# Nine stages fused into three blocks, the third scan's spreads reordered, gate products on half rows, and the position table loaded earlier

## The reference

```python
x = _L0(x)   # window attention (8x8 windows, 8 heads) + MLP 64-256-64 (gelu), a layernorm before each
x = _L1(x)   # bias, 12x12 FIR up by 2, leaky relu, clip, 12x12 FIR down by 2
x = _L2(x)   # selective scan over 8 tokens of each pixel, both directions; then
             #   y = (ys * gelu(z)) @ W_out ; group norm of y ; return x + y
x = _L3(x)   # see below

# _L3, with 4 chunks of 16 channels, L = 1024 pixels
xn = layer_norm(x)
xi, z = split(xn_chunk @ in_w.T)
xc = silu(causal_conv4(xi) + conv_b)
h  = exp(dt*A) * h + (dt*xc) B      # per pixel, 32 channels x 16 states
y  = (sum_s h*C + xc*Dp) * silu(z)
ym = y @ out_w.T + skip_scale * xn_chunk
tm = layer_norm(ym) @ proj_w.T + proj_b
out = x + tm
return out + fc2(gelu(fc1(out))) + x
```

## Time and profile before

| | |
|---|---|
| median of three executions | 1917.81 us (1914.59 to 1926.75) |
| the profiled execution, own time | 1923.28 us |
| its span (first to last instruction) | 1921.2 us |
| mean granted tensor clock | 0.932 of full |
| busy: PE, DVE, ACT, POOL | 1538.0, 1544.9, 1204.6, 1076.6 us |
| third scan: first to last scan of DVE starts | 1343.2 to 1811.6 us |

### The profile page before, as it was taken

One profiled execution on the slowest core, in us unless ns is written; L12 is line 12 of the kernel. 1 busy time (PEld: TensorE's weight loads), 2 busy tenths in 40 slices (PEclk: granted clock), 3 DMA queues, 4 the chain that ended last, 5 costly groups with the idle time before them and its releaser, 6 DMA issues. The chain is left out here.

```text
span 1921.2 us, 29107 instructions
## 1 busy us (share of the span) xinstructions
PE 1538.0 (80%) x9958; PEld 788.5 (41%) x9958; DVE 1544.9 (80%) x1256; ACT 1204.6 (63%) x1855; POOL 1076.6 (56%) x700
## 2 busy tenths in 40 slices
PE   5999887998887788878887876668787788777687
PEld 2666545885333333333333333234333333333233
DVE  3787655555899999999999999443999999999754
ACT  4666584435676767667767664366667766766356
POOL 1777401000577777777777775100989889888401
PEclk8999998998899999998999998778999999999799
DMA  4000000000444444444454454100000000000001
GB/s 142 3 0 0 1 1 1 1 1 1 77 93 95 92 94 93 93 94 92 87 98 91 94 97 90 37 1 1 1 1 1 0 0 0 0 0 1 12 1 44
DMA packets 23295, 78.08 MB, mean 41 GB/s; under 512 B 3776, under 2 KB 4672, under 8 KB 22976
## 3 DMA queue, kind: packets, MB, share of 16 engines
q0 software_dynamic: 18288, 66.59, 18.3%
q1 hardware_dynamic: 4944, 10.68, 1.9%
HBM read 8.58 MB, written 2.10 MB: 6 GB/s over the span
## 5 line engine op out<-in xcount | busy, mean ns | idle before, releaser
L1288 POOL TENSOR_TENSOR s_prod<-s_ahead,s_cs 128x1024 f32<-128x1024 f32 x127 | 309.1, 2434 | 185.6 <-DVE s_back L1231 157.2
L1909 POOL TENSOR_TENSOR r_state<-r_state,r_cs 128x1024 f32<-128x1024 f32 x127 | 300.7, 2376 | 187.5 <-DVE r_state L1860 187.5
L1860 DVE TENSOR_TENSOR_SCAN r_state<-r_decay,r_pu 128x1024 f32<-128x1024 f32 x128 | 292.7, 2287 | 26.9 <-PE r_py L1706 23.0
L1228 DVE TENSOR_TENSOR_SCAN s_ahead<-s_fore,s_pu 128x1024 f32<-128x1024 f32 x128 | 292.7, 2287 | 9.2 <-ACT s_fore L1145 2.3
L1231 DVE TENSOR_TENSOR_SCAN s_back<-s_aft,s_pu 128x1024 f32<-128x1024 f32 x128 | 289.5, 2262 | 1.3 <-ACT s_aft L1155 1.3
L1779 ACT ACTIVATE r_decay<-r_pd,r_aneg 128x1024 f32<-128x1024 f32 x128 | 142.8, 1116 | 122.6 <-PE r_pd L1650 122.2
L1145 ACT ACTIVATE s_fore<-s_pd,s_aneg 128x896 f32<-128x896 f32 x128 | 130.0, 1016 | 111.3 <-PE s_pd L958 110.3
L1650 PE MATMUL r_pu<-r_partsu,selr 64*128 64x512 f32 x512 | 156.7, 426 | 41.8 <-DVE r_state L1860 36.9
L1856 DVE TENSOR_TENSOR r_pu<-r_pu,r_bs 128x1024 f32<-128x1024 f32 x128 | 155.2, 1213 | 12.8 <-PE r_pu L1650 12.4
L958 PE MATMUL s_pu<-s_partsu,selr 64*128 64x512 f32 x512 | 100.0, 469 | 76.6 <-DVE s_back L1231 73.4
L1221 DVE TENSOR_TENSOR s_pu<-s_pu,s_bs 128x1024 f32<-128x1024 f32 x128 | 154.6, 1208 | 4.8 <-PE s_pu L958 4.8
(11 more groups left out here) (345 smaller groups left out, 3285.8 us busy)
## 6 DMA issues: line engine op xcount, KB each, us to landing
s_ahead<-s_back POOLq DMA_DIRECT2D x127, 512.0 KB, 4.6
x_act<-in_x_dram SPq DMA_DIRECT2D x8, 256.0 KB, 5.5
out_dram<-x_act SPq DMA_DIRECT2D x16, 128.0 KB, 2.4
k_fir<-in_pack_fir_dram SPq DMA_DIRECT2D x1, 1600.0 KB, 10.6
k_scan<-in_pack_scan_dram SPq DMA_DIRECT2D x1, 1600.0 KB, 13.9
k_l<-in_pack_l_dram SPq DMA_DIRECT2D x1, 515.0 KB, 3.5
k_l<-in_pack_l_dram SPq DMA_DIRECT2D x1, 450.0 KB, 14.6
k_ln<-in_pack_ln_dram SPq DMA_DIRECT2D x3, 131.0 KB, 2.8
```

The costliest lines, as they stand in the source:

```text
L1228: dve.tensor_tensor_scan(ahead[:, v % 4], f, feed[:], 0.0, ALU.mult, ALU.add).then_inc(ahead_done, 1)
L1288: pool.tensor_tensor(prod[:, b], ahead[:, v % 4], cs[:, buf].rearrange("p i n -> p (i n)"), ALU.mult).then_inc(prod_done, 1)
L1860: dve.tensor_tensor_scan(state[:, v % 4], decay[:, v % 4], feed[:], 0.0, ALU.mult, ALU.add).then_inc(scanned, 1)
L1909: pool.tensor_tensor(state[:, v % 4], state[:, v % 4], cs[:, phase, q // 2], ALU.mult).then_inc(multiplied, 1)
```

## The change

1. `rel` is a tensor of the first block; `load` issues its 16 transfers on SP behind x and the attention constants, ahead of the other constants. In `attention` DVE scales the query bias first and copies the table after it.
2. `gated`: each half's product uses only its own 64 rows, at its own row position of the array, and the two stand side by side with one semaphore step; four banks and four gate buffers.
3. `normed_mlp` holds n2 and m0 in one block, and n4, `project3` and m3 in another. `normed_convolve3` holds `groupnorm`, n3 and `convolve3`. Averages run one chunk behind; the first chunk is split inside the norm's loop; weights are prepared at its start; activation tables are loaded by name ahead of the loops; of the group norm's four scalings POOL makes the last two.
4. `scan3`: the eight spreads of a group move from one per step to `SLOTS`: none in steps k = 0 and 1, two in k = 2 and k = 6. `r_place` moves behind the sums, one in k = 6 and one in k = 0. ACT's Ln moves from k = 2 to k = 1.

The diff, cut to its core:

```diff
@@ attention
-            dve.wait_ge(rel_in, 16 * HALVES * WS)
+            dve.tensor_scalar(bq_scaled[:], c["bq"], float(HD) ** -0.5, None, ALU.mult).then_inc(bq_done, 1)
+            dve.wait_ge(rel_in, 16 * HALVES * WS)
             dve.tensor_copy(bias[:], rel[:, ::-1, :].rearrange("p j h -> p h j")).then_inc(bias_done, 1)
@@ gated, tensor
+            for k in range(CHUNKS + 1):
+                if k < CHUNKS:
+                    wait(pe, gate_done, 2 * k - 2)
+                    for h in range(HALVES):
+                        rows = slice(h * C, (h + 1) * C)
+                        mm = pe.matmul(ps_z[2 * k % 4 + h][:], c["wz"][rows, h * P:(h + 1) * P],
+                                       src[rows, k * N:(k + 1) * N], start=True, stop=True, tile_position=(h * C, 0))
+                    mm.then_inc(z_done, 2)
@@ normed_mlp, tensor
+            for n in range(CHUNKS + 1):
+                if n < CHUNKS:
+                    wait(pe, norm_done, n - 3)
+                    pe.matmul(center[n % 4][:], ln["center"], src[:, n * N:(n + 1) * N], start=True,
+                              stop=True).then_inc(centered, 1)
...
+                if project and n >= 3:
...
+                    pe.matmul(ps_proj[k % 2][:], c["wpj"], xn[:, k * N:(k + 1) * N], start=True,
+                              stop=True).then_inc(proj_done, 1)
@@ normed_mlp, scalar: norm loop, then
+                if n == CHUNKS - 3:
+                    high(0)
+            act.preload_act_table_set("gelu_and_others")
+            for n in range(CHUNKS):
+                if n + 1 < CHUNKS:
+                    high(n + 1)
@@ normed_mlp, vector: behind the norm of chunk n
+                if project and n >= 2:
+                    mix(n - 2)
+            if project:
+                low(0)
+                mix(CHUNKS - 2)
+                mix(CHUNKS - 1)
@@ normed_convolve3, tensor
+                    pe.wait_ge(x_done, n * N // HW + 1)
+                    wait(pe, norm_done, n - 3)
@@ normed_convolve3, vector
+            add(0)
+            add(1)
...
+            for n in range(CHUNKS):
+                if n == CHUNKS - 2:
+                    low(0)
+                    low(1)
...
+                if n in (1, 2):
+                    add(n + 1)
@@ normed_convolve3, gpsimd
+            for bl in range(2, BL):
+                pool.tensor_scalar(scaled[:, bl], src[:, bl * HW:(bl + 1) * HW], gain[:, bl:bl + 1],
+                                   offset[:, bl:bl + 1], ALU.mult, ALU.add).then_inc(scaled_late, 1)
@@ scan3
+        SLOTS = [0], [1], [2, 3], [4], [], [], [5, 6], [7]
...
-                    if k == 2 and live(s, UNITS):
+                    if slot == 5 and live(s, UNITS):
                         pe.wait_ge(lo_bc, gi + 8)
...
+                if z % 8 in (2, 4) and live(o, UNITS):
+                    phase, chunk = cells(z)[1], z % 8 // 4
+                    pe.matmul(ps_y[:], place[:, 2 * phase + chunk], xc[:, columns(o - z % 16 + 8 * chunk, N)],
+                              start=False, stop=False, skip_group_check=True)
@@ scan3, scalar, k == 1
+                    act.wait_ge(one_done, gi + 8)
+                    act.activation(ln[:], one[:], ACT.Ln).then_inc(ln_done, 8)
```

More of the change, by code:

```diff
@@ L1415, in _ @@
[L1415 to L1422 removed]
+            act.wait_ge(const_in, 16)
@@ new lines, in _ @@
+            act.preload_act_table_set("gelu_and_others")
+            for n in range(CHUNKS):
+                if n + 1 < CHUNKS:
+                    high(n + 1)
+                wait(act, tot_done, n - 1)
+                for unit in range(4):
+                    k = unit % 2
+                    act.wait_ge(hid_done, 4 * n + unit + 1)
+                    act.activation(act_out[:, n % 2, unit], hidden[unit][:], ACT.Gelu,
+                                   bias=c["b1"][:, k:k + 1]).then_inc(gelu_done, 1)
@@ L1444, in convolve3, with low @@
-def convolve3(nc, consts, xn, xc):
+            dve.wait_ge(ln_in, 16)
+            dve.wait_ge(w1_hi, 1)
+            dve.tensor_tensor(w1[:, 1], c["w1"], w1[:, 0].bitcast(F32), ALU.subtract).then_inc(w1_lo, 1)
+            dve.tensor_tensor(bias[:], c["b2"], c["l1b"], ALU.add).then_inc(bias_done, 1)
+            def low(n):
+                dve.wait_ge(hi_done, 2 * n + 2)
+                wait(dve, hid_done, 4 * (n - 1))
+                for h in range(HALVES):
+                    split(dve, hidden_src[:, n * N:(n + 1) * N], parts[:, n % 2, h], h, True).then_inc(lo_done, 1)
@@ L1446, in convolve3, with _, normed_convolve3 @@
+        @block.gpsimd
+        def _(pool):
+            if project:
+                for n in range(CHUNKS):
+                    cols = slice(n * N, (n + 1) * N)
+                    pool.wait_ge(mixed_done, n + 1)
+                    pool.tensor_tensor(x[:, cols], mixed[:, cols], x[:, cols], ALU.add).then_inc(resid_done, 1)
+def normed_convolve3(nc, consts, src, sums, x, xn, xc):
     with ExitStack() as ctx:
         m = Scope(nc, ctx)
+        g, g_in = consts["l2post"]
+        ln, ln_in = consts["ln"]
@@ L1453, in convolve3 @@
+        centered, squared, var_done, logged, rstd_done, norm_done, out_done = (
+            m.sem("c_" + t) for t in ("centered", "squared", "var", "logged", "rstd", "norm", "out"))
         folded_done, w_hi, w_lo, zeroed, hi_done, lo_done, conv_done, silu_done = (
@@ L1692, in body @@
                         wait(pe, y_done, o - 1)
-                    if z % 8 == 3:
-                        for chunk in range(2):
-                            pe.matmul(ps_y[:], place[:, 2 * phase + chunk],
-                                      xc[:, columns(o - z % 16 + 8 * chunk, N)], start=False, stop=False,
-                                      skip_group_check=True)
                     if isinstance(o, int) and o == UNITS - 1:
@@ L1938, in _, with load @@
             skewed3(pool, body)
-def load(block, dram, x, arrived, consts, tiles):
+def load(block, dram, x, arrived, consts, tiles, rel, rel_in):
     @block.sync
```

464 lines of the change are left out of this document (248 added, 216 removed).

## The result

The changed kernel takes 1863.85 us, the median of 4 runs (1857.59 to 1871.68), against 1916.20 (1913.13 to 1926.75, 4 runs): ratio 0.973, 95% interval 0.970 to 0.976. I had predicted 1861. The profiled execution took 1861.92 us (span 1860.1), 61.1 us of span less than the one before; medians moved by 52.4. So about 9 us of the difference between the two traces is taken as chance, and part of what follows is to find out where.

The account below looks back on a forecast made before the run. No engine bounds the whole; each stage has its own limit. Gains of 6.7, 11.0, 3.7, 10.0, 11.7 and 13.4 sum to 56.5 us: from profiled 1923.28 to 1866.8, less 5.5 for that execution, 1861 us; range 1843 to 1885.

Parts of the forecast that it names:

- Table: Start of attention: with the query bias ahead of the table, ACT starts at once, a gain of 6.7 us.
- n2 and m0: Second norm and first MLP in one block: the second product's first matmul comes earlier, a gain of 3.7 us.
- gate stages: Both gate stages: a chunk takes 2.2 us, 0.7 less, as row pairs overlap; 5.5 us a stage, 11.0 for both.
- The rival without overlap: Gate stages: row pairs don't overlap, PE keeps 2.93 us a chunk; 11 us more, 1872; chance 0.07.
- Table switches: ACT's table loads: counted as 1.28 us each; the rival adds a drain to each, 4 us more, 1865; chance 0.03.
- Group norm and convolution: Group norm, n3 and convolution: earlier first square, faster norm loop and earlier unit 2; 10.0 us, with 8 and 12 as ends.
- Third scan: Third scan: 10 us in 13 groups, 2.0 from the last group's place products, 0.3 given back; 11.7 us.
- Tail: Fourth norm's first matmul to the MLP's first second product: PE-bound norm loop, load and split under projections; gain 13.4 us.
- The tail's own sign: Tail: 27.7 us instead of 41.1 from the norm's first matmul to the second product.
- the spreads' order gives nothing: Third scan: the longer chain at k = 2 eats what k = 0 and 1 give back; 10 more, 1871; chance 0.17.
- fell in every group: Third scan: PE's clock falls in all 14 groups, as PE idles twice at k = 2; 13.5 more, 1874; chance 0.13.
- the rival in which it stays up: Third scan: PE's clock stays up and five waits lose 1.3 to 1.5 us each; 7 less, 1854; chance 0.13.

Follow-up runs that it names:

- e1: The changed kernel with the whole third scan put back as before: 1876.73 us, ratio 0.979.

## Why the prediction came out right, and where it did so by luck

- **Table, n2 and m0, gate stages** (6.7, 3.7, 11.0): right. Undoing the gates gives 5.4 a stage, for the reason named: the pair by rows overlaps as the pair by columns does (1.13 and 1.08 us for four passes). I had DVE as the bound of a chunk, at 2.1 to 2.2; it is PE, at 2.07. The rival without overlap is out, and the trace of before spoke against it: "no row has an f32 pair side by side by rows", I wrote, but the third scan's jobs are pairs of products of 64 rows, of values rounded beforehand, and their passes start together.

```profile
1498.08 0.39 PE L1650 MATMUL r_pu<-r_partsu,selr 64*128 64x512 f32 x1
1498.09 0.39 PE L1650 MATMUL r_pd<-r_partsd,selr 64*128 64x512 f32 x1
```

- **Table switches**: 1.28 us each and no more. The one that starts at 1259.39 shows it: ACT's next instruction starts 0.01 us behind its end. The rival fell. No drain shows in front of that load either: ACT's Exp ends 0.02 us ahead of it. By the rule of the Trainium skill that the prediction names (ScalarE: Activation LUTs, What ACT_TABLE_LOAD costs), which adds a drain of about 1.38 us, the trace does not agree, and the measurement decides.
- **Group norm and convolution** (10.0): 8.7. The first square came 4.8 us earlier (my 4.5), the last Exp ended 32.5 us behind the first group norm product (my 32.1), the wait for the third add was the 2 us I gave. Unit 2 of the convolution started 1 us later than I had worked out, 1262.50 for 1261.5: behind the load ACT and then DVE had still to split its input.
- **Third scan** (11.7, of it 10 for the order, 2 for the place products): the sum is too small, and the reasons are wrong. The place products bring 15 to 16 us, order and Ln 1.4 to 2. I had read that PE arrives late at k = 2, and blamed "each step held a spread, its copy, and a product in the same bank" at k = 0 and 1. But the lateness begins at k = 7, with 1.88 us of place products ahead of a sum for which a scan waits; the 0.2 us at scan 6 in my own list of losses was its sign. I left that loss standing ("that at k = 7 (0.2) stays") and looked at the place products in the last group only. And the 0.75 us a group that I kept for k = 2 and 3 are 0.25.
- **The clock in the third scan.** My sum left it as it was, my rivals put it at none or at all groups. It fell at k = 2 in 4 of 13 where before it had fallen in 5, and a fall cost 1.3 to 2.5 us instead of 1.5: 7.9 us together, 7.7 before. The Trainium skill (TensorE: Matmul & The Clock Gate, A second HAM failure mode: psum-queue depth-cycling) says that short idle times between groups of matmuls make the clock swing. By that rule the traces agree in part: with the 1.4 us gap filled no group of four traces shows a long wait, but with the gap open most groups show none either, and e1 shows none at all.
- **Tail** (13.4): 8.3 in this execution, 9.5 in the six traces that start at full clock (31.6). The term left out 2.9 us: DVE's splits and its last x_norm beside POOL's residuals, which I had placed there myself ("no longer end a block"), at durations from rows where POOL was still. Of the 1.0 us that is left, half is the norm's loop: I had its last Exp end 19.6 us behind the first matmul (1868.5), and it ends at 20.1. The other half lies between there and the second product. The tail's own sign, 27.7 us, was missed, with 32.8. The Trainium skill has a rule that I did not use (SBUF — State Buffer, Who interferes with whom): a DVE instruction with two SBUF inputs contends with a GpSimd instruction that reads SBUF, a copy or tensor_scalar in its two-port modes contends with GpSimd too, and one with a single SBUF input outside these modes does not. By that rule the traces agree: the mixing, with one input in PSUM, stays at 0.75 beside POOL's additions in before (three in a row in 2.47 us), and x_norm and the splits do not keep their times.

```profile
1871.40 2.47 DVE L1532 SCALAR_TENSOR_TENSOR mixed<-j_ps,k_l3post,x_act 128x512 f32<-128x512 f32 x3 [0.75 <-PE j_ps L1523]
...
1872.23 1.27 POOL L1540 TENSOR_TENSOR x_act<-mixed,x_act 128x512 f32<-128x512 f32 x1 [0.24 <-DVE mixed L1532]
```

- So 1861 came close by luck in part: the scan's surplus of 5 us, with 2.8 us of chance at its start, made up for the tail's 5 and the convolution's 1; and the medians of before and after lie closer together than the two traces. Inside the scan two wrong terms cancelled, 2 us for the place products that bring 15 to 16 and 10 for an order that brings 1.4 to 2. The rival "the spreads' order gives nothing" (chance 0.17) was nearly right about the order, yet its 10 us more did not come, since the place products had brought them. The clock neither stayed up nor fell in every group. That the time of the rival in which it stays up, 1854, is what filling the gap gives (1853) is chance too, since 2.4 us of that gain are the shorter chain at k = 2.

## What to carry to other kernels

When an engine is late in a periodic loop, look back along it for the step at which the lateness starts: the waits appear where the slack ends, several steps behind the cause. Here one long pair of matmuls ahead of an awaited sum cost 15 to 16 us over 14 groups, and the reordering of the spreads, aimed at the place where the waits showed, brought 1.4 to 2. Work whose place is free belongs where its engine waits for another; here that also ended the waits that came with a fallen clock. And a duration read from a stage in which the other vector engine was still does not hold where fusing puts the two side by side.

## What the runs showed of the hardware

- TensorE's clock falls within a loop at waits of 1.4 and 0.7 us in some groups and not in others with the same instructions, and is back at full speed by the end of the next sum. With the first wait cut to 0.5 us it did not fall at that place in 52 groups, though once elsewhere. Idle times of 1.0 to 1.1 us in other steps of the same loop brought none in the kernel after. A matmul whose result is needed anyway did as filler.
- The same code starts at 1.2 or 2.4 GHz from one execution to the next where a stage begins after a pause: four passes of the fourth norm in 1.95 or in 3.2 to 3.65 us, eight of the gate stage in 5.41 or 6.40, the way from the group norm to the first scan in 86.8 or 90.5. Such starts are the likeliest cause of the 9 us by which the traces differ more than the medians; before has but one trace, so this stays an estimate.
- DVE and POOL reading SBUF at once: DVE's pair of 64x512 splits 1.40 us alone, 2.36, 2.91 and 3.30 beside POOL; its 128x512 x_norm 0.55 alone and 0.99; POOL's 128x512 addition 1.27 alone and 1.76. DVE's addition with one input in PSUM keeps its 0.75 beside POOL.
- Two float32 products of 64 rows side by side, 512 columns each, take 1.13 us together, where two of 128 rows take 1.98.
- A table load on ACT takes 1.28 us, and the work on both sides follows within 0.02 us.
